# Both channel blocks of a pair in one scan and one product of a Mamba layer, cut by a zero decay between them

## What is computed

```python
def step(h, inp):
    d_t, u_t, b_t, c_t = inp
    dA = jnp.exp(d_t[..., None] * A)
    h = dA * h + (d_t * u_t)[..., None] * b_t[:, None, :]
    y = jnp.einsum('bdn,bn->bd', h, c_t)
    return (h, y)
```

## Time and profile before

| | |
|---|---|
| runs | 1638.37 us median of 3 (1637.38 to 1647.46) |
| profiled execution | span of 1636.5 us, first to last instruction; no time outside the span is given for it |
| busy in the span | PE 1336.6, DVE 797.4, ACT 904.6, POOL 402.9 us |
| scan stage | 49 to 661 us of the span |
| DMAs of rows B and C | 128 of 512 KB, 3.7 us from issue to landing (median) |
| mean granted TensorE clock | 0.899 |

### The profile page before, as it was taken

One profiled execution on the slowest core, in us unless ns is written; L12 is line 12 of the kernel. 1 busy time (PEld: TensorE's weight loads), 2 busy tenths in 40 slices (PEclk: granted clock), 3 DMA queues, 4 the chain that ended last, 5 costly groups with the idle time before them and its releaser, 6 DMA issues.

```text
span 1636.5 us, 15496 instructions
## 1 busy us (share of the span) xinstructions
PE 1336.6 (82%) x5511; PEld 628.7 (38%) x5511; DVE 797.4 (49%) x1213; ACT 904.6 (55%) x1164; POOL 402.9 (25%) x177
## 2 busy tenths in 40 slices
PE   6477566887598748896735999999999988979999
PEld 2122123343334324653521223223223234568887
DVE  3899989989998899216520002001011016461011
ACT  3536444654466436122435997998998944751310
POOL 0637655654455466015030000000000001000000
PEclk9588787999789878998756999999999988989999
DMA  5323332332243233102994000000000000011701
GB/s 184 118 78 129 129 115 86 122 116 77 82 138 116 77 128 116 45 8 49 102 112 39 1 1 1 1 1 0 0 0 0 0 0 1 1 52 35 325 14 39
DMA packets 35633, 107.96 MB, mean 66 GB/s; under 512 B 3650, under 2 KB 14146, under 8 KB 32915
## 3 DMA queue, kind: packets, MB, share of 16 engines
q1 hardware_dynamic: 35572, 107.19, 23.7%
HBM read 93.60 MB, written 2.36 MB: 59 GB/s over the span
## 4 chain that ended last, share of the span: by engine, by line
PE 47%; DVE 24%; ACT 13%; issue 8%; DMA 5%; SPq 1%; POOL 1%; DVEq 0%; ACTq 0%; POOLq 0%
DVE ps L864 13%; PE ps L1558 10%; PE ps L1543 9%; ACT arena L706 6%; PE ps L1362 4%; PE ps L1667 4%; DMA arena<-arena 4%; PE ps L1708 3%; PE ps L1317 3%; DVE arena L875 2%; PE ps L1685 2%; PE ps L1696 2%; PE ps L1248 2%; SPq L377 1%; PE ps L1588 1%
## 5 line engine op out<-in xcount | busy, mean ns | idle before, releaser
L706 ACT ACTIVATE arena<-ps,bound 128x1024 f32<-128x1024 f32 (+1 forms) x416 | 421.1, 1215 | 26.7 <-PE ps L1543 26.7
L431 POOL TENSOR_TENSOR arena<-arena 128x1024 f32<-128x1024 f32 x128 | 300.7, 2353 | 262.0 <-DVE ps L864 218.1
L864 DVE TENSOR_TENSOR_SCAN ps<-ps,arena 128x512 f32<-128x512 f32 x256 | 327.3, 1279 | 18.1 <-ACT ps L567 13.7
L1317 PE MATMUL ps<-arena,ident 128*128 128x512 f32 x452 | 245.1, 683 | 106.1 <-POOL arena L437 66.1
L567 ACT ACTIVATE ps<-arena 128x512 f32<-128x512 f32 x256 | 173.1, 689 | 269.1 <-DVE arena L882 175.5
L1543 PE MATMUL ps<-arena 97*128 (+3 forms) x832 | 218.9, 385 | 22.8 <-issue 20.7
L1558 PE MATMUL ps<-arena 128*32 128x512 f32 (+1 forms) x1664 | 222.8, 607 | 1.1 <-ACT arena L706 0.9
L1317 PEld LDWEIGHTS ps<-arena,ident 128*128 128x128 f32 x452 | 91.5, 214 | 243.3 <-issue 89.0
L1141 DVE COPY arena<-ps 128x512 f32<-128x512 f32 x16 | 11.1, 691 | 355.8 <-PE ps L1558 355.8
L419 POOL TENSOR_TENSOR rstd<-ve,mhalf 128x4 f32<-128x4 f32 (+3 forms) x18 | 23.5, 1308 | 625.0 <-DVE ve L1166 469.9
L875 DVE TENSOR_TENSOR arena<-ps,arena 128x512 f32<-128x512 f32 x256 | 171.4, 669 | 0.0
(11 more groups left out here) (178 smaller groups left out, 1386.5 us busy)
## 6 DMA issues: line engine op xcount, KB each, us to landing
arena<-bc_scratch SPq DMA_DIRECT2D x128, 512.0 KB, 3.7
arena<-in_mw SPq DMA_DIRECT2D x16, 1024.0 KB, 8.7
arena<-arena SPq DMA_DIRECT2D x48, 128.0 KB, 14.8
arena<-arena SPq DMA_DIRECT2D x12, 400.2 KB, 16.4
arena<-in_w SPq DMA_DIRECT2D x2, 1024.0 KB
out<-xt SPq DMA_DIRECT2D x4, 512.0 KB, 2.9
xt<-in_x SPq DMA_DIRECT2D x1, 1536.0 KB
arena<-in_ctx SPq DMA_DIRECT2D x1, 1200.8 KB, 7.8
```

The source lines that it names most:

```text
L431: pool.tensor_tensor(dbu[:, w % DR], du[:, DP * p:DP * p + DP], over(bg[:, w // BG % 2, n % BG], DP), ALU.mult).then_inc(S["dbu_ready"], 1)
L706: act.activation(flat(prob[0:n, v % 2, 2 * h:2 * h + 2]), ps[0:n, 2 * (r % 3):2 * (r % 3) + 2, :].rearrange("p a b -> p (a b)"), ACT.Exp, ...
L864: dve.tensor_tensor_scan(decay_bank(w, x), decay_bank(w, x), dbu[:, w % DR, x], carry[:, d, n:n + 1], ALU.mult, ALU.add).then_inc(S["scan_ ...
L1317: last = mm(bank(x), ident[:, :], state(2 * j + s)[:, x], start=False, stop=(j % HP == HP - 1 and (j in SUMMED or s == 1)))
```

## The change

The two instructions of a step's scan become one over 1024 columns, 128 partitions, both banks of the pair in a row; so do the two products. So that the second block doesn't go on from the first's last state, its first decay must be zero: after delta x u is formed, the first column of delta of the pair's second block is overwritten by `CUT` (1e28), and its exponential with a negative A (at most -`LEAST`) is zero. What the true first decay would have carried over is kept apart: ScalarE computes the 16 true first decays of the second block (`head_decays`, i = 9 and 28), VectorE multiplies them by the carried states into `handed` and writes `CUT` (`step_heads`, i = 10 and 29), and GpSimd adds the step's column of it to the first element of the second block in `dbu`, in an instruction of its own behind the product. The first block's carried state still comes in as the scan's start. The copy of the last columns moves to ScalarE, ahead of the decays two steps on. `between` now stands between the scan and the product of one step. Semaphore counts are adapted.

```diff
+CUT = 1e28
+LEAST = 1e-26
...
-                    sp.wait_ge(S["dbu_ready"], BG * (q - 1))
+                    sp.wait_ge(S["dbu_ready"], 2 * BG * (q - 1))
-                    sp.wait_ge(S["hc_ready"], DP * BG * (q - 1))
+                    sp.wait_ge(S["hc_ready"], BG * (q - 1))
...
                 c, p, n = step(w)
                 if n == 0:
                     pool.wait_ge(S["du_ready"], c * DP + p + 1)
+                    pool.wait_ge(S["head_ready"], 2 * (c * DP + p) + 1)
                 if n % BG == 0:
                     pool.wait_ge(b_in[w // BG % 2], 16 * (w // BG // 2 + 1))
                 if w >= DR:
-                    pool.wait_ge(S["scan_done"], DP * (w - DR + 1))
+                    pool.wait_ge(S["scan_done"], w - DR + 1)
                 pool.tensor_tensor(dbu[:, w % DR], du[:, DP * p:DP * p + DP], over(bg[:, w // BG % 2, n % BG], DP),
                                    ALU.mult).then_inc(S["dbu_ready"], 1)
+                pool.wait_ge(S["dbu_ready"], 2 * w + 1)
+                pool.tensor_tensor(dbu[:, w % DR, 1, 0:1], dbu[:, w % DR, 1, 0:1], handed[:, p, n:n + 1],
+                                   ALU.add).then_inc(S["dbu_ready"], 1)
             def add_pair(j):
-                pool.wait_ge(S["hc_ready"], DP * (2 * j + 2))
+                pool.wait_ge(S["hc_ready"], 2 * j + 2)
                 pool.tensor_tensor(state(2 * j), state(2 * j), state(2 * j + 1), ALU.add).then_inc(S["pair_ready"], 1)
             def layer_norm_root(c):
...
+            def head_decays(c, p):
+                h = c * DP + p
+                act.wait_ge(S["delta_ready"], h + 1)
+                if h >= 2:
+                    act.wait_ge(S["head_ready"], 2 * (h - 1))
+                act.activation(first_decay[:, p], neg_a[:, DP * p + 1], ACT.Exp,
+                               scale=delta[:, DP * p + 1, 0:1]).then_inc(S["sp_act"], 1)
+
+            def carry_over(w):
+                c, p, n = step(w)
+                act.wait_ge(S["hc_ready"], w + 1)
+                if c + 1 < NC:
+                    if n == 0 and c:
+                        act.wait_ge(S["head_ready"], 2 * (c * DP + p) + 2)
+                    act.activation(carry[:, DP * p:DP * p + DP, n:n + 1],
+                                   ps[:, 2 + DP * (w % 2):2 + DP * (w % 2) + DP, C - 1:C],
+                                   ACT.Copy).then_inc(S["carry_done"], 1)
+                    act.wait_ge(S["carry_done"], w + 1)
             def decays(w):
                 c, p, n = step(w)
                 if n == 0:
-                    act.wait_ge(S["delta_ready"], c * DP + p + 1)
+                    act.wait_ge(S["head_ready"], 2 * (c * DP + p) + 2)
+                if w >= 2:
+                    carry_over(w - 2)
                 for x in range(DP):
                     d = DP * p + x
-                    if w >= 2:
-                        act.wait_ge(S["hc_ready"], DP * (w - 2) + x + 1)
-                        if x == 0:
-                            act.wait_ge(S["carry_done"], w - 1)
                     act.activation(decay_bank(w, x), delta[:, d], ACT.Exp,
                                    scale=neg_a[:, d, n:n + 1]).then_inc(S["da_ready"], 1)
...
-            dve.tensor_scalar(flat(neg_a), flat(neg_a), -1.0, None, ALU.mult).then_inc(S["prep_dve"], 1)
+            dve.tensor_scalar(flat(neg_a), flat(neg_a), -1.0, -LEAST, ALU.mult, ALU.min).then_inc(S["prep_dve"], 1)
...
+            def step_heads(c, p):
+                h = c * DP + p
+                dve.wait_ge(S["sp_act"], h * 5 + 5)
+                if c:
+                    dve.wait_ge(S["carry_done"], (c - 1) * NU + (p + 1) * NS)
+                dve.tensor_tensor(handed[:, p], first_decay[:, p], carry[:, DP * p + 1], ALU.mult).then_inc(S["head_ready"], 1)
+                dve.wait_ge(S["du_ready"], h + 1)
+                dve.memset(delta[:, DP * p + 1, 0:1], CUT).then_inc(S["head_ready"], 1)
+
+            def scan(w):
                 c, p, n = step(w)
-                d = DP * p + x
-                if x == 0:
-                    dve.wait_ge(S["dbu_ready"], w + 1)
-                    if w >= NU:
-                        dve.wait_ge(S["carry_done"], w - NU + 1)
-                dve.wait_ge(S["da_ready"], DP * w + x + 1)
-                dve.tensor_tensor_scan(decay_bank(w, x), decay_bank(w, x), dbu[:, w % DR, x],
-                                       carry[:, d, n:n + 1], ALU.mult, ALU.add).then_inc(S["scan_done"], 1)
-
-            def times_c(w, x):
+                dve.wait_ge(S["dbu_ready"], 2 * (w + 1))
+                if w >= NU:
+                    dve.wait_ge(S["carry_done"], w - NU + 1)
+                dve.wait_ge(S["da_ready"], DP * (w + 1))
+                dve.tensor_tensor_scan(decay_banks(w), decay_banks(w), flat(dbu[:, w % DR]),
+                                       carry[:, DP * p, n:n + 1], ALU.mult, ALU.add).then_inc(S["scan_done"], 1)
+
+            def times_c(w):
                 c, p, n = step(w)
-                if x == 0 and n % BG == 0:
+                if n % BG == 0:
                     dve.wait_ge(c_in[w // BG % 2], 16 * (w // BG // 2 + 1))
-                if x == 0 and w >= 2 * RING:
+                if w >= 2 * RING:
                     dve.wait_ge(S["y_acc"], w // 2 - RING + 1)
-                dve.wait_ge(S["scan_done"], DP * w + x + 1)
-                dve.tensor_tensor(state(w)[:, x], decay_bank(w, x), cg[:, w // BG % 2, n % BG],
-                                  ALU.mult).then_inc(S["hc_ready"], 1)
-
-            def carry_over(w):
-
-                c, p, n = step(w)
-                dve.wait_ge(S["scan_done"], DP * (w + 1))
-                dve.tensor_copy(carry[:, DP * p:DP * p + DP, n:n + 1],
-                                ps[:, 2 + DP * (w % 2):2 + DP * (w % 2) + DP, C - 1:C]).then_inc(S["carry_done"], 1)
+                dve.wait_ge(S["scan_done"], w + 1)
+                dve.tensor_tensor(state(w), ps[:, 2 + DP * (w % 2):2 + DP * (w % 2) + DP, :],
+                                  over(cg[:, w // BG % 2, n % BG], DP), ALU.mult).then_inc(S["hc_ready"], 1)
...
+                if i == 10:
+                    step_heads(c, 1)
+                    if i == 29:
+                        step_heads(c + 1, 0)
...
             step_sum(0, 0)
             step_size(0, 0)
             step_channels(0, 0)
+            step_heads(0, 0)
             dve.wait_ge(S["w_mamba"], 16 * 6)
             for w in range(NW_ALL):
-                scan(w, 0)
-                if w >= 1:
-                    times_c(w - 1, 1)
+                scan(w)
                 between(w // NU, w % NU)
-                scan(w, 1)
-                times_c(w, 0)
-                carry_over(w)
-            times_c(NW_ALL - 1, 1)
+                times_c(w)
             second_residual(NC - 2)
             gated(NC - 1, 1)
             second_mean(NC - 2)
...
                     pe.wait_ge(S["pair_ready"], SUMMED.index(j) + 1)
                 for s in range(1 if j in SUMMED else 2):
                     for x in range(DP):
-                        if j not in SUMMED:
-                            pe.wait_ge(S["hc_ready"], DP * (2 * j + s) + x + 1)
+                        if x == 0 and j not in SUMMED:
+                            pe.wait_ge(S["hc_ready"], 2 * j + s + 1)
                         last = mm(bank(x), ident[:, :], state(2 * j + s)[:, x], start=False,
                                   stop=(j % HP == HP - 1 and (j in SUMMED or s == 1)))
                 last.then_inc(S["y_acc"], 1)
```

More of the change, by code:

```diff
@@ L175, in decoder_layer @@
         zs = m.take(2, DB, C)
+        first_decay = m.take(2, NS)
+        handed = m.take(2, NS)
         junk = h1t.rearrange("p a b -> p (a b)").rearrange("p (a b) -> p a b", b=DM)
@@ L256, in decoder_layer @@
 mark1 st1 ve1 rs1 a0_ready a0t_ps a0t_ready z_ps u_ps u_raw z_ready hist_in conv_step u_ready
-            xdbl_ps xdbl_ready bc_stored b_even b_odd c_even c_odd dt_ps sp_in sp_act sp_step delta_ready
+            xdbl_ps xdbl_ready bc_stored b_even b_odd c_even c_odd dt_ps head_ready sp_in sp_act sp_step delta_ready
             du_ready da_ready dbu_ready scan_done carry_done hc_ready pair_ready y_acc skip_done
@@ L287, in decay_bank, with decay_banks @@
             return bank(2 + DP * (w % 2) + x)
+        def decay_banks(w):
+            return banks(2 + DP * (w % 2), DP)
         def work(x):
@@ L548, in step_exp @@
                 h = c * DP + p
-                act.wait_ge(S["sp_act"], h * 4 + 2)
+                act.wait_ge(S["sp_act"], h * 5 + 2)
                 act.activation(flat(sp_exp), flat(sp_exp), ACT.Exp, scale=-1.0).then_inc(S["sp_act"], 1)
@@ L553, in step_log @@
                 h = c * DP + p
-                act.wait_ge(S["sp_act"], h * 4 + 3)
+                act.wait_ge(S["sp_act"], h * 5 + 3)
                 act.activation(flat(sp_ln), flat(sp_exp), ACT.Ln, bias=1.0).then_inc(S["sp_act"], 1)
+            def head_decays(c, p):
[15 more added lines that the diff above has]
```

(22 more changed lines are left out.)

## The result

The changed kernel takes 1682.74 us in the median of four runs (1675.37 to 1691.52), against 1638.10 before: a ratio of 1.0264 with a 95% interval of 1.0218 to 1.0309. 1676 was predicted. Each kernel has executions some 10 us longer than its others, and a lower mean clock goes with them: of before, over all sets, 10 of 90 (1645.8 to 1648.0 us, the others at most 1640.9), of after 6 of 8 (1687.2 to 1691.5, mean clock 0.879 to 0.883, the other two 1675.4 and 1678.2 at 0.887).

The account below looks back on a forecast made before the run. VectorE's own time was taken to bound the stretch from 49 to 661 us. Terms of -8.6 and +46.9 us for collisions made +38 on a span of 1636.5, the median 1.9 above it: 1676 us, range 1638 to 1694.

Parts of the forecast that it names:

- The mechanism: In `between`: a pending GpSimd product goes ahead of VectorE's second operation, which waits about 2.0 us; +46.9 us in all.
- no collisions: Rival at the second operation of each `between`: no collision cost is paid, -8.6 us, 1630 us; chance 0.14.
- half of them: Rival: collisions only where the second operation of `between` waits for a semaphore, +20, 1658 us; chance 0.14.
- GpSimd as the bound: Rival: GpSimd's small add takes 1.0 us, so 3.7 us per step; +12 on the forecast, 1688 us; chance 0.10.
- a long scan that saves nothing: Rival on VectorE: the joint scan saves nothing, 27 us dearer than taken, 1700 us; chance 0.04.
- 54 - 6.0 + 2.4: Collisions in `between`: 27 x 2.0 = 54, less 6.0 already paid on these lines, plus 2.4 for the small add.
- the 27 places listed: Second operations of `between` expected to wait for GpSimd's product, 2.0 us each, 54 us together.
- the term of -3.5 us: Two or three collisions fall where VectorE would have waited for a decay anyway: -3.5 us.
- 46.9: Net cost in us of VectorE's collisions with GpSimd in `between`, after what is already paid or covered.
- -8.6 us: All terms but collisions: VectorE's steps -21.3, added waits and uncollected gains +3.9, +1.8, +4.3, heads +1.2, start +1.5.
- 21.3: VectorE's gain in us from joint scans and products: 57 bare steps at 0.10, 71 steps with work at 0.22.
- 3.9, 1.8 and 1.5: Added waits in us: three longest ScalarE chains 3.9, nine smaller waits 1.8, GpSimd's later first product at the start 1.5.

Follow-up runs that it names:

- Experiment 1: The changed kernel with GpSimd's product released by the product by C (hc_ready) instead of the scan: 1644.66 us, ratio 1.0017.
- the second set: The changed kernel run again unaltered, for a second profile: 1688.38 us, ratio 1.0309 against before.
- experiment 7: The changed kernel with GpSimd released by the product by C, `turned_h1` at i = 21 and pair 1's step sizes later: 1633.44 us, 0.9972.
- experiment 9: The kernel of experiment 7 with the carry copy on VectorE behind the product by C instead of on ScalarE: 1630.46 us, 0.9949.
- experiment 10: The kernel of experiment 9 without sums of pairs on GpSimd (`SUMMED = []`): 1631.39 us, 0.9958.

## Why the prediction was right, point by point

**The mechanism** was the forecast one. The rivals fall: no collisions (taps and L877 grew), half of them (L938 pays three times as the third of four, where by the code only the first of the four waits), GpSimd as the bound (its small add takes 0.250 us in the mean), a long scan that saves nothing (2.349).

**Collisions**, 54 - 6.0 + 2.4 = 50.4 us gross: the excess grew by 49.4. Of the 27 places listed 25 pay; not listed were two L859 held by a pair sum and an L833 and an L938 that stood first. Twelve convolutions were named and all twelve pay, by 7 taps and 5 times L845: three stand behind delta x u at i = 9, as listed, and two at i = 10 behind L893 of the heads, which takes the first place in front of the convolution and which I had left out. So L849's mean is 1.133 and not 1.3. L877 is hit 4 times, as said, up to 3.18. GpSimd's mean went to 2.561, 0.04 short of what I had asked for. The Trainium skill, "SBUF — State Buffer", section on who interferes with whom, has the loser blocked for the whole instruction; 2.35 for each was to be compared with 2.0. The longest tap lost 1.97 us (2.721 less 0.752), the longest L845 2.20; the trace speaks for the shorter, somewhat over the 2.0 taken for L845.

**What of it was covered**: the term of -3.5 us was mis-sized. Undoing the collisions gave back 36.1 us of a 46.5 us excess, so some 10 were covered and not 3.5; the net cost is 36, not 46.9.

**The rest of the change**, -8.6 us, was mis-sized the other way. Experiment 1, nearly free of new collisions (17.3 us of excess for 14.4), still has a stage 6.2 us longer than before. Its own later release has little part in that: it waits 5.0 us for GpSimd's product (L439) at two scans, but without the small add the same two scans wait 1.9 and 2.2 us for ScalarE. Two terms of it can be sized. The bare steps take 3.59 to 3.63 us, a gain of 0.01 to 0.02 in the mean and not 0.10: the product starts 0.13 us after the scan ends, not 0.04,

```profile
202.83 2.35 DVE L904 TENSOR_TENSOR_SCAN ps<-ps,arena 128x1024 f32<-128x1024 f32 x1
...
205.31 1.23 DVE L915 TENSOR_TENSOR arena<-ps,arena 128x1024 f32<-128x1024 f32 x1
206.46 2.35 DVE L904 TENSOR_TENSOR_SCAN ps<-ps,arena 128x1024 f32<-128x1024 f32 x1
```

while a step with one operation gains 0.25 (4.76 to 4.51), so 57 x 0.02 + 71 x 0.25 = 18.9 us at most for 21.3. And the waits in front of scans: 7.2 us was put down for all added waits (3.9, 1.8 and 1.5), and the rows of after have 7.3 (25.1 less 17.8); but in experiment 1, without the collisions, 33.7 stand there, 15.9 more than before: 9.6 for ScalarE and 6.3 for GpSimd. As far as these two runs show, the terms fitted only because collisions hid the rest. The small add on GpSimd was taken at 0.45 us, dear by 0.2.

**The sum** of the stage was +38.3 for a measured 42.3; two errors, some 11 us too much for collisions and 15 too little for the rest, nearly cancel. That the sum came so near was luck; its parts were not as good.

**Outside the sum**: I wrote that nothing of the change reaches what follows the stage. That failed: what follows took 10.9 and 10.3 us longer in the two profiled executions, nearly all of it at TensorE's lower clock. That is most of the distance from 1676 to the 1688.4 of the second set. Its cause stays open.

**The rule that a semaphore costs nothing** (the Trainium skill, "VectorE: DVE Perf Modes", section on the DRAIN) would have made a bare step 3.40 us. It is 3.59 to 3.63, so the trace speaks against it: 0.13 us behind a dependence, against 0.08 before the end without.

## What to carry to other kernels

When instructions of one engine are put in another order, look at what the other engines start on its semaphores: here one release moved by a scan cost 36 us, and one line that ties it to the product took that back. Merging two instructions saves their fixed part, but a dependence that the old order had bridged comes bare and takes nearly all of it where no other work stands between. A gain or loss in a stage is the kernel's only after the stretch behind it is compared as well, since TensorE's granted clock there can take 10 us of it.

## What was not expected of the hardware

- A GpSimd product of two SBUF tiles beside a scan with its decays in PSUM costs neither anything (2.35 and 2.35 us, in experiment 1). Beside VectorE operations on SBUF alone, a pending one goes ahead of the next VectorE instruction: where it started beside the first of two, the second took 1.96 to 2.20 us longer.
- GpSimd's addition of one element takes 0.19 us alone (0.250 in the mean), and up to 1.05 us beside a VectorE operation on SBUF (experiment 7). ScalarE's copy of two columns from PSUM takes 0.171.
- The clock granted to TensorE behind the stage was 0.79 and 0.78 in the two profiled executions of after, 0.93 in before. Around the first projection it was 1.00 in experiment 9 and 0.77 in experiment 10; the same work up to the feed-forward's end took 12.3 us more.
